# A fused attention and feed-forward layer on one core: the first transposes of a step directly behind the scores, and the fill between them in two parts

## The reference

```
q = x Wq^T (32 heads of 128), rotary on q
k = low-rank keys (8 KV heads) with a rotated part, v = low-rank values
scores = q k^T / sqrt(128), causal mask, softmax, out = attn v, then out Wo^T
x = layernorm(x + attention)
x = layernorm(x + (silu(x W1^T) * (x W3^T)) W2^T)     W1, W2, W3 unpacked from 4 bits with scales
```

## Time and profile before

| | |
|---|---|
| median of 3 runs | 2386.08 us (2385.03 to 2389.29) |
| the profiled execution's own time | 2387.51 us |
| its span, first to last instruction | 2385.7 us |
| mean granted TensorE clock over the span | 0.998 |
| stage A with the first query heads, ends at about | 226 us |
| stage B, 16 turns of about 111 us (107 the first, 110 the last), ends at about | 1998 us |
| stage C, to the end | 388 us |

### The profile page before, as it was taken

One profiled execution on the slowest core, in us unless ns is written; L12 is line 12 of the kernel. 1 busy time (PEld: TensorE's weight loads), 2 busy tenths in 40 slices (PEclk: granted clock), 3 DMA queues, 4 the chain that ended last, 5 costly groups with the idle time before them and its releaser, 6 DMA issues.

```text
span 2385.7 us, 41133 instructions
## 1 busy us (share of the span) xinstructions
PE 2370.0 (99%) x12028; PEld 1993.1 (84%) x12028; DVE 1427.1 (60%) x3780; ACT 1621.0 (68%) x3221; POOL 578.6 (24%) x453
## 2 busy tenths in 40 slices
PE   9999999999999999999999999999999999999998
PEld 7888888888888888888888888888888888888886
DVE  5334766666767676766666676767676674242332
ACT  4224878888888888887878888888888885122211
POOL 3002323233332323232323333232323220000000
PEclk9999999999999999999999999999999999999999
DMA  7867444434353444444434445354434435311110
GB/s 273 300 216 289 131 143 138 136 132 155 131 176 110 170 138 141 132 141 149 136 129 139 148 135 174 106 171 138 148 127 145 137 129 209 120 71 36 53 35 18
DMA packets 133255, 340.24 MB, mean 143 GB/s; under 512 B 13328, under 2 KB 30736, under 8 KB 122640
## 3 DMA queue, kind: packets, MB, share of 16 engines
q1 hardware_dynamic: 133200, 339.53, 42.2%
HBM read 232.00 MB, written 111.67 MB: 144 GB/s over the span
## 4 chain that ended last, share of the span: by engine, by line
PE 96%; issue 1%; DVE 1%; ACT 1%; DMA 1%; SPq 0%; POOL 0%; DVEq 0%; POOLq 0%
PE b_ps L267 45%; PE b_sps L267 34%; PE b_tps L1549 10%; PE b_ps L1608 3%; PE b_tps L1608 2%; PE b_tps L267 1%; DMA b_xs<-xs_d 0%; DMA a_raw<-in_wkrT 0%; PE b_sps L1558 0%; ACT b_pt L1050 0%; ACT b_sc L1035 0%; ACT b_sc L1029 0%; DVE c_n_stats L286 0%; DVE b_sc L1252 0%; DVE a_xs L1176 0%
## 5 line engine op out<-in xcount | busy, mean ns | idle before, releaser
L1270 DVE TENSOR_TENSOR b_pt<-b_tps,b_pt 128x512 fp32r<-128x512 f32 (+3 forms) x768 | 426.8, 556 | 301.6 <-ACT b_pt L1050 297.5
L267 PE MATMUL b_sps<-b_kt,b_qs 128*128 128x512 f32 (+4 forms) x2304 | 497.1, 343 | 0.2
L1035 ACT ACTIVATE b_sc<-b_sc,b_rinv 128x896 f32<-128x896 f32 (+7 forms) x512 | 396.1, 774 | 105.4 <-DVE b_rinv L1260 99.5
L267 PEld LDWEIGHTS b_sps<-b_kt,b_qs 128*128 128x128 f32 x2304 | 403.1, 188 | 55.8 <-issue 1.4
L1050 ACT ACTIVATE b_pt<-b_tps 128x512 fp32r<-128x512 f32 (+3 forms) x768 | 366.9, 478 | 119.1 <-PE b_tps L1549 117.6
L267 PE MATMUL b_ps<-b_xs,b_wq 128*128 128x512 f32 x1536 | 441.0, 407 | 0.5 <-DMA b_xs<-xs_d 0.5
L267 PE MATMUL b_ps<-b_pt,b_vt 128*128 128x512 f32 x1584 | 436.0, 402 | 0.3 <-DVE b_ys L1281 0.3
L267 PE MATMUL b_ps<-b_wo,b_ot 128*128 128x512 f32 x1536 | 423.9, 405 | 0.1
L1029 ACT ACTIVATE b_sc<-b_sc,b_nmax 128x896 f32<-128x896 f32 (+7 forms) x512 | 395.5, 772 | 40.2 <-DVE b_nmax L1252 37.1
L1252 DVE CUSTOM_DVE_ANT_0 b_sc<-b_sps,b_mask 128x896 f32<-128x896 f32 (+7 forms) x512 | 386.7, 755 | 16.1 <-PE b_sps L267 16.0
L1549 PE MATMUL b_tps<-b_ident,b_sc 128*128 128x128 f32 x2304 | 374.3, 272 | 1.4 <-DVE b_pt L1270 1.4
(11 more groups left out here) (133 smaller groups left out, 2271.9 us busy)
## 6 DMA issues: line engine op xcount, KB each, us to landing
b_xs<-xs_d SPq DMA_DIRECT2D x32, 2048.0 KB, 9.1
b_ys<-y_d SPq DMA_DIRECT2D x128, 256.0 KB, 2.7
y_d<-b_ys SPq DMA_DIRECT2D x128, 256.0 KB, 3.0
k_d<-a_ks SPq DMA_DIRECT2D x32, 512.0 KB, 3.9
v_d<-a_vs SPq DMA_DIRECT2D x32, 512.0 KB, 3.1
b_kt<-k_d SPq DMA_DIRECT2D x64, 256.0 KB, 4.5
b_vt<-v_d SPq DMA_DIRECT2D x16, 1024.0 KB, 4.9
b_wraw<-in_wqT SPq DMA_DIRECT2D x64, 256.0 KB, 2.7
```

Source lines behind the costliest of these rows:

```text
L267: ins = nc.tensor.matmul(out, *every[n], start=(n == 0), stop=(n == len(every) - 1))
L1035: nc.scalar.activation(sc[:, slot, 0:w], sc[:, slot, 0:w], ACT.Copy, scale=rinv[:, slot:slot + 1])\
L1270: nc.vector.tensor_tensor(pt[:, u, LO, 0:nj, h * P:(h + 1) * P], tps[n % 2][:, 0:nj], pt[:, u, HI, 0:nj, h * P:(h + 1) * P], ALU.subtract) ...
```

## The change

Two tables are changed:

```diff
-PE_ORDER = (("scores", "fill", "fill", 0, "fill", 1),
-            ("fill", "scores", 0, "fill", "fill", 1),
-            ("scores", "fill", 0, "fill", 1, "fill"),
-            ("scores", "fill", 0, "fill", 1, "fill"))
-
-SHARES = ((1,), (0, 1), (1, 1.25, 1))
+PE_ORDER = (("scores", "fill", 0, "fill", 1),
+            ("fill", "scores", 0, "fill", 1),
+            ("scores", 0, "fill", 1, "fill"),
+            ("scores", 0, "fill", 1, "fill"))
+
+SHARES = ((1,), (0, 1), (1, 1))
```

## The result

The changed kernel takes 2393.43 us (median of 7 runs, 2392.95 to 2394.10); the kernel before, run beside it, 2386.62 us (7 runs). The ratio of the fast runs is 1.0026, with an interval of 1.0016 to 1.0036, some 6 us slower; one of the seven runs of before took 8483.18 us and is not in the ratio, and the two medians as they stand differ by 6.8 us. The profiled execution of the changed kernel took 2393.43 us, 5.9 us more than the one of before, with a span of 2391.6 us and the same granted clock, 0.998.

The account below looks back on a forecast made before the run. TensorE bounds the kernel, busy 2370.0 of 2385.7 us. Terms 5.3 + 3.3 + 0.5 + 0.7 = 9.8 us on the profiled 2387.51 give 2397.3, which stands 1.4 above the median: 2395.9 us, range 2390.0 to 2401.5.

Parts of the forecast that it names:

- the forecast's own terms: Whole kernel: the summed losses with their own spread, 7.3 to 13.6 us, so 2393.4 to 2399.7 us.
- rival A: Stalls spread: steps 1, 2 and last turn pay fully, thin margins of steps 20, 29 break; 16.5 us, 2402.6; chance 0.12.
- rival B: Helpers come earlier too, DVE's chain of step 20 shifts by the shortfall; 4.3 us, 2390.4; chance 0.15.
- Switches at nothing: PE's switches between kinds of products: no price of their own, taken as 0.
- Steps 19 to 31: First transposes directly behind the scores wait for DVE in step 21; shortfalls over 15 turns sum to 5.3 us.
- the 0.15 us between DVE's end and the start of T0: First transpose group: one that really waits starts 0.15 us after DVE's subtraction ends.
- Steps 1 and 2: Four fills instead of six ahead of the first transposes; larger shortfall over 15 turn starts sums to 3.3 us.
- The last turn: Steps from 19 on: two fills no longer cover a wait, lost once; 0.5 us, between zero and 4.3.
- Restarts: Four transposes after a wait take 0.38 us against 0.36; 37 waits at 0.02 us, 0.7 us.
- the 2 us kept for the range: Possible gain from fewer switches, 0.01 us each over 13 steps of 16 turns; minus 2 us.
- the profile's signs: PE waits for DVE some 40 times, 8 to 11 us, three places; turn 0.5 to 0.7 us longer; ACT idle below 117.6.

Follow-up runs that it names:

- f2: Changed kernel with two fills ahead of the first transpose group in steps 19 to 21; 2388.34 us, ratio 1.0009 to the kernel before.
- e1: Kernel before with the new order in steps 1 and 2 alone; 2388.46 us, ratio 1.0005 to the kernel before.
- e3: Kernel before with the new order in steps 19 to 23 alone; 2391.22 us, ratio 1.0019 to the kernel before.
- f3: f2 with the order and shares of the kernel before in steps 0 to 2; 2387.71 us, ratio 1.0002 to the kernel before.
- f5: Changed kernel with ACT's copy of the second group ahead of the weights in steps 16 to 23; 2390.80 us, ratio 1.0016 to before.
- e4: Changed kernel with the two waits ahead of a transpose group exchanged, DVE's subtraction first; 2394.28 us, ratio 1.0032 to the kernel before.

## Why the prediction was right, and where its terms were off

The sign and the range held: 2393.43 us, between 2390.0 and 2401.5, and slower by 0.26%. The forecast of 2395.9 was 2.5 us too high, and the sum of 9.8 us stands against 5.9 between the two profiled executions. 2393.43 lies at the lower end of what the forecast's own terms allowed, 2393.4. By its steps:

1. **The mechanism holds.** A start that was held by DVE is known by two marks: it follows DVE's end closely, and the first transpose then lasts 0.30 us or more in place of 0.27. In the loop of after 48 starts have both, at 0.055 to 0.084 us: step 1 in 14 turns, step 2 in 13, step 21 in 13, and T1 of step 20 in 8. (5 more come within 0.17 us of DVE's end without the longer transpose.) None stands in steps 24 to 31 of the loop (rival A), and step 21 did not go away by itself (rival B). f2 removes the loss of steps 20 and 21 by two fills alone.
2. **Switches at nothing**: right, by steps 21 and 22 of f2.
3. **Steps 19 to 31, 5.3 us forecast.** Measured, with restarts: 14 times 0.331 in the loop and 0.37 in turn 0, 5.0 us. Of it PE stands still for 3.7 us, and the late first products (below) are some 1.2. The term that was mis-sized is the 0.15 us between DVE's end and the start of T0. It was read where PE does wait in the trace of before, in the last turn; in the loop it is 0.056 us (42 of the 48 starts are at 0.055 to 0.057). That takes 0.09 from each of 14 shortfalls, 1.3 us; turn 0 is outside the loop and does pay 0.147. In turn 7 the forecast 0.33 us becomes 0.24, and 0.22 are measured at T0 (1.27 less 1.05 us). That single turn agrees because the weights landed there at nearly the same place. Turn by turn the reading did not hold: turn 8, forecast as the worst with 0.60 us, loses 0.34, and so does turn 11, forecast with 0.02. The copy of the weights started 1.44 and 0.86 us behind the scores of step 20 in those two turns of before, and 1.23 in both after. The forecast read the DMA's landings in one execution; that their sum came out near in another is in part luck.
4. **Steps 1 and 2, 3.3 us forecast.** In the loop steps 1 to 4 together lose 0.125 us a turn, 1.75 us, or 2.4 us at the 0.17 that leave out turn 13; in turn 15 steps 2 and 3 lose some 0.5 more, of which 0.36 stand at a fill behind T0 for which the profile names no releaser. Here too 0.09 us per wait was too much: turn 7 loses 0.04 us of standing still at step 1 where 0.14 was forecast. What the argument missed besides is that the loop of before already waits, in step 3, and that a gain can lie there. The rows of before, turn 7, in order of time:

```profile
1006.10 0.69 DVE L1270 TENSOR_TENSOR b_pt<-b_tps,b_pt 128x512 fp32r<-128x512 f32 x1
...
1006.85 0.14 PEld L1549 LDWEIGHTS b_tps<-b_ident,b_sc 128*128 128x128 f32 x1
1006.85 0.33 PE L1549 MATMUL b_tps<-b_ident,b_sc 128*128 128x128 f32 x1
```

DVE ends at 1006.79 and the transpose starts 0.06 us later, in each of turns 1 to 14, with no idle time printed beside it. With T0 and T1 of step 2 earlier, this wait goes and step 3 is 0.148 us shorter (0.150 in e1, 0.146 in f2, nothing in e3 and f3, which keep the old start). Step 4 gives 0.102 of that back: its second fill now comes up to DVE's addition at L1281 before that has freed its bank. Before and after, turn 7:

```profile
1008.95 0.81 PEld L267 LDWEIGHTS b_ps<-b_pt,b_vt 128*128 128x128 f32 x4
...
1009.11 1.08 PE L267 MATMUL b_ps<-b_pt,b_vt 128*128 128x512 f32 x4
```

```profile
1011.33 0.69 DVE L1281 TENSOR_TENSOR b_ys<-b_ps,b_ys 128x512 f32<-128x512 f32 x1
...
1011.84 0.48 PE L267 MATMUL b_ps<-b_xs,b_wq 128*128 128x512 f32 x1
...
1012.14 0.77 PEld L267 LDWEIGHTS b_ps<-b_pt,b_vt 128*128 128x128 f32 x4
1012.16 1.18 PE L267 MATMUL b_ps<-b_pt,b_vt 128*128 128x512 f32 x4
```

   The fill at 1012.16 starts 0.14 us after DVE's end at 1012.02. It comes 0.32 us behind the one ahead of it, as it did before; but its load starts only 0.02 us ahead of it, where that was 0.16, and the next fill comes 0.09 us later than before in the mean (0.321 us behind it in place of 0.230).
5. **The last turn, 0.5 us forecast**: its steps 22 to 30 are 0.06 us longer together, and from the start of the turn to the end of the program it is 0.3 us more. So next to nothing was lost there, the lower end that the forecast named.
6. **Restarts, 0.7 us forecast**: too low for one wait. In the loop four transposes behind a wait take 0.412 us to the next fill in the mean in place of 0.355, and the first of them lasts 0.33 us in place of 0.27. The forecast's 0.38 was read in the last turn, and there it is right: 0.383, with 0.30 for the first. So both prices were taken outside the loop, and they err in opposite ways. From DVE's end to the next fill a wait costs 0.15 + 0.38 = 0.53 us there and 0.056 + 0.412 = 0.47 in the loop, 0.06 us less. The kernel before has 14 such waits in its loop already, in step 3, so that the change adds 34 there; their restarts are some 2 us more. Most of this stands in the differences of points 3 and 4. For a load of 128 columns the Trainium skill gives 107 ns ("TensorE: Matmul & The Clock Gate", "LDWEIGHTS (loading the stationary operand)"). Here a load lasts 0.14 us, and 0.06 us at most are exposed at a wait. The rows above have the product starting 0.00 to 0.02 us behind the start of its load, which agrees with another sentence of the same page ("Architectural detail: the array is 16× 32×32, not 1× 128×128"), that a product can begin before the load is complete.
7. **Not forecast**: steps 22 to 26 come 0.052 us a turn earlier, 0.7 us in all, and in f3, where the chain of step 21 is not late, 0.074. Which wait of before this removes is not shown; it is far within the 2 us kept for the range.

Of the profile's signs, the number of waits was near (some 40 forecast, 48 in the loop, where before has 14), and so were the three places. The other signs were off. By its own words the prediction is wrong if PE's waits stay near 1.4 us, and in PE's list they do, at 1.2: the 8 to 11 us do not appear there, since idle times this short are not in the list. That sign could not have told the cases apart, and the load's list and the starts do. A turn is 0.40 us longer and not 0.5 to 0.7. ACT's idle time for transposes fell from 117.6 to 106.8 us and was worth nothing, as forecast.

What stays open: no version tried is faster than the kernel before; f3 can't be told from it. Putting T1's copy first (f5) on top of two fills ahead was not tried, and neither was an earlier issue of the weights' DMA.

## What to carry to other kernels

On an engine that is 99% busy, the distance between work that fills a buffer's slot and the work that needs the slot is worth keeping: before moving a group earlier, subtract its new start from the end of what frees its buffer, turn by turn, and put a piece of independent work of that size ahead of it (here two fills, 0.46 us, remove the loss of steps 20 and 21). Where that end hangs on a transfer, its place in one turn of one execution is a sample: read the spread over turns, and not the worst turn's name. Read short waits (here up to 0.24 us) from starts, against the end of what they wait for, and not from the idle time of the busy engine. Take the price of a wait from the same place in the program, since it depends on which instruction carries it. Judge small changes by the length of the repeated part, step by step: steps that nothing disturbs agree here within some 0.01 us in single profiles whose ends differ by several us, and for a step that now and then waits for a transfer the median is the better reading.

## What the runs showed of the hardware that was not expected

- What a wait of PE costs behind DVE's end depends on the instruction that carries it. From DVE's end to the start of the transposes it is 0.056 us where the load of the product carries DVE's wait (the loop of before and after; e4 outside the loop and in steps 20 and 21 in it), 0.131 us where an ALU_OP ahead of it has it (e4, steps 1 and 2, 25 starts), and 0.147 us where an EVENT_SEMAPHORE ahead has it (before and after, outside the loop, 9 starts at 0.146 or 0.147 in after).
- The first transpose after such a wait takes 0.33 us to its modelled end in place of 0.27 where the load carries the wait, and the next fill is 0.06 us late; with the EVENT_SEMAPHORE it takes 0.30 us, and the fill is 0.03 us late. A fill of 512 columns behind a wait (step 4 of after) puts the next one back by 0.09 us.
- A wait of PE of up to 0.24 us leaves at most 0.08 us of idle time in PE's rows: PE's list has 4 waits for DVE in the whole kernel, where the starts show 48 in the loop alone, and PE's busy time grew by 5.1 us where the span grew by 5.9.
- The DMA of the query weights lands at another place in each turn: the copy that waits for it starts 0.86 to 1.44 us behind the scores of step 20 in the loop of before, and 0.88 to 1.46 in that of after.
